# Softmax scaling moved behind the values, and heads' slots taken in twos, in an attention and expert kernel

## The chip, the cores and the metric

The kernel runs on one core of one Trainium2 chip. The metric is device time in microseconds (us). Engines in the text: PE is TensorE (PEld its weight loads), DVE is VectorE, ACT is ScalarE, POOL is GpSimd, SP is SyncE, which here only issues DMAs.

## What is computed

A block of layer norm, causal attention with 16 heads of 64 and rotary positions, and an expert layer whose output gates the attention. x is 8 x 256 x 128, all fp32.

```python
xn = layernorm(x)
q = xn @ wq.T;  lat = xn @ w_kv_down.T            # 16 heads of 64; latents of 64
k = lat @ w_k_up.T;  v = lat @ w_v_up.T
q, k = rope(q), rope(k)
probs = softmax(q @ k.T / 8 + causal)             # per head, 256 x 256
s = (probs @ v).reshape(B, S, 1024) @ wo.T
e_star = max(top2(xn @ gate_w + gate_b))          # one expert a token
g = silu(2 * (gelu(xn @ w1[e_star] + b1[e_star]) @ w2[e_star] + b2[e_star]))
out = x + s * g
```

## The kernel before, in words

The program is written engine by engine: `program` (L286) calls, on each engine, `start`, then `slot(g)` for g = 0 to 63, and between slots 39 and 40 `finish` and `experts`. The order on an engine is the order in which its functions write it; engines wait for each other by semaphores. Nothing else sets it.

A **slot** g is one pair of heads of one batch row (8 batches of 8 pairs); i in the names is the head within the pair. The 256 queries are two chunks: the first 128 (k = 0) see 128 keys, the others (k = 1) see 256. So a head's rows are 128 + 256 = 384 columns wide; the first 128 are called the corner here. In a slot:

- PE `scores(g + 2)` (L1074, L1080 for the 256 columns, L1082 for the corner) into s_bank[i]; it waits until slot g + 1's maxima are taken. The two heads lie in two halves of the rows (64*128 tiles).
- PE `project` (L1058): item m is four heads' q (m even, L1054 to L1056) or k (m odd, L1070, L1071); `items(g)` puts item g + 6 in slot g, and two of them in the slots of TWICE (36, 38).
- DVE `row_max(g + 2)` (L588, L594): mask, negated maximum and copy to `masked`, four instructions. Then `denominators(g + 1)` (L601), the reciprocal of the row sums, and `rotate` (L581, L585) of the item, which multiplies by cos and sin; POOL `rotated` (L457, L463) adds the halves into `staged`, and SP `place` (L356, L363) copies two items to `qk_sb` by four DMAs.
- ACT `exponentials(g + 1, i)` (L880, L885) with row sums, into `pexp`, double buffered.
- `scale(g + 1)` turns pexp into `probs`: four instructions, on POOL (L474), some on DVE (L612) and ACT (L898) in slots in which POOL also issues indirect DMAs.
- PE `turn(g)` (L1085, L1092): six transposes of probs into t_bank[i]; ACT `turned_probs(g)` (L901, L907) copies them to `probsT`, four slots deep.
- PE `values(g)` (L1095, L1106, L1108) multiplies by the latents into o_bank, one slot at a time up to slot 23 (`ALONE`), two slots at once after; ACT `ctx_out` (L909, L914) copies o_bank to `ctxT`; PE `output(g)` (L1111, L1120) adds the pair's share of the block's result in y_bank.
- In slots 22 to 37 POOL scatters a tile of tokens into `sorted_x` in DRAM (L482), in slots 43 to 58 it gathers the gates (L490). SP's `load` (L423, L425) brings sorted_x back into z in two pieces, 4 tiles and 18 tiles, in slot 38. DVE `finalise(b)` (L763) multiplies a batch's result by its gate and adds x, in the slots of FINALS; it reads y_keep or, from batch 5 on, y_bank.

`experts` runs 22 tiles of 128 tokens (PE L1257, L1285, L1300; ACT L1038 gelu; POOL L549 copies the expert's first weights, DVE L854 and L867). Its second tile waits for both loads of z (`t == 1`, L1295).

## Time and profile before

| | us |
|---|---|
| median of 3 runs | 309.83 (309.74 to 309.87) |
| the profiled execution | 310.5 |
| its span, first to last instruction | 308.7 |
| granted TensorE clock over the span | 0.998 |

| engine | busy us | share of the span |
|---|---|---|
| PE | 294.3 | 95% |
| PEld | 235.4 | 76% |
| ACT | 242.9 | 79% |
| DVE | 221.0 | 72% |
| POOL | 215.9 | 70% |

The chain of work that ended last is PE for 64%, POOL for 12%, DVE for 8% and ACT for 2% of the span; 11% is issue. Matmuls are pipelined: the row of one is longer than its pace, so the distance from start to start tells what it costs. A timeline row of several instructions (x4, x6) merges them. Busy time is the union of such rows.

### The profile page before, as it was taken

What the parts mean: (1) busy time and instruction counts of PE and PEld (TensorE: products, weight loads), DVE (VectorE), ACT (ScalarE), POOL (GpSimd) and SP (SyncE); (2) the same over time, 40 slices, a digit from 0 to 9 for tenths busy, and PEclk for the clock granted to TensorE, in tenths of its full rate; (3) what the DMA queues carried; (4) which work ended last, traced back from release to release, by engine and by line L of the source; (5) the groups of instructions that cost most, each with busy time, mean ns of one, the idle gap of its engine ahead of it and who ended that gap; (6) DMA issues with size and microseconds to landing.
All of it is one profiled execution on the core that took longest, in us unless ns stands there. A gap on an engine that the chain in (4) does not pass through costs nothing.

```text
span 308.7 us, 8487 instructions
## 1 busy us (share of the span) xinstructions
PE 294.3 (95%) x2362; PEld 235.4 (76%) x2362; DVE 221.0 (72%) x883; ACT 242.9 (79%) x851; POOL 215.9 (70%) x321
## 2 busy tenths in 40 slices
PE   8897999999999999999999989999989999899994
PEld 3566878888888888777777789999867777786763
DVE  3889998987787998988887523323278789898651
ACT  3387889898887889999897665555799999889982
POOL 3378878786786879999999933332138999889730
PEclk9999999999999999999999999999999999999999
DMA  6764595979333333333345470000063334344200
GB/s 204 232 140 112 107 308 124 225 168 302 74 69 71 68 71 89 92 87 87 99 104 134 129 197 0 2 2 0 3 187 71 93 102 115 103 108 133 71 19 17
DMA packets 39596, 33.35 MB, mean 108 GB/s; under 512 B 4801, under 2 KB 36674, under 8 KB 39554
## 3 DMA queue, kind: packets, MB, share of 16 engines
q1 hardware_dynamic: 38098, 30.51, 38.3%
q0 software_dynamic: 1024, 2.10, 2.5%
q8 instruction: 20, 0.33, 0.4%
q10 hardware_dynamic: 432, 0.23, 0.3%
q14 instruction: 22, 0.18, 0.2%
HBM read 11.07 MB, written 4.98 MB: 52 GB/s over the span
## 4 chain that ended last, share of the span: by engine, by line
PE 64%; POOL 12%; issue 11%; DVE 8%; ACT 2%; DMA 1%; POOLq 1%; SPq 0%; DVEq 0%; ACTq 0%
PE bank L1092 9%; PE bank L1080 8%; PE bank L1106 7%; PE bank L1120 6%; PE bank L1285 6%; PE bank L1300 6%; POOL probs L474 5%; POOL staged L463 4%; PE bank L1054 3%; DVE rot_out L585 3%; PE bank L1108 3%; PE bank L1082 3%; DVE masked L594 2%; PE bank L1188 2%; PE bank L1070 2%
## 5 line engine op out<-in xcount | busy, mean ns | idle before, releaser
L885 ACT ACTIVATE pexp<-masked,negmax 128x128 f32<-128x128 f32 (+1 forms) x256 | 114.1, 452 | 1.5 <-DVE negmax L594 1.4
L474 POOL TENSOR_SCALAR probs<-pexp,rden 128x256 f32<-128x256 f32 (+1 forms) x184 | 80.3, 451 | 26.0 <-DVE rden L601 23.3
L594 DVE CUSTOM_DVE_ANT_0 masked<-bank,mask 128x128 f32<-128x128 f32 (+1 forms) x256 | 75.9, 351 | 27.1 <-PE bank L1082 26.9
L463 POOL TENSOR_TENSOR staged<-rot_out 128x512 f32<-128x512 f32 x63 | 80.2, 1275 | 17.8 <-DVE rot_out L585 17.3
L585 DVE TENSOR_TENSOR rot_out<-bank,rot 128x1024 f32<-128x1024 f32 x64 | 77.6, 1214 | 4.0 <-PE bank L1056 2.7
L907 ACT COPY probsT<-bank 128x384 f32<-128x384 f32 x128 | 54.9, 480 | 22.9 <-PE bank L1092 21.9
L1092 PE MATMUL bank<-ident,probs 128*128 128x128 f32 x384 | 54.7, 275 | 1.8 <-ACT probsT L907 0.9
L885 ACT ACTIVATION_READ_ACCUMULATOR pexp<-masked,negmax 128x1 f32 x256 | 49.9, 195 | 0.0
L1080 PE MATMUL bank<-qk_sb 64*128 64x256 f32 x256 | 45.0, 427 | 2.9 <-DVE negmax L594 2.1
L1092 PEld LDWEIGHTS bank<-ident,probs 128*128 128x128 f32 x384 | 43.1, 140 | 5.2 <-POOL probs L474 1.9
L1120 PE MATMUL bank<-vo_sb,ctxT 128*128 128x128 f32 x256 | 39.4, 278 | 0.7 <-ACT ctxT L914 0.7
L1038 ACT ACTIVATE probsT<-bank,w_own 128x128 f32<-128x128 f32 x88 | 25.1, 367 | 18.8 <-PE bank L1285 18.8
L1106 PE MATMUL bank<-probsT,lat_all 128*64 128x256 f32 (+1 forms) x184 | 37.7, 488 | 0.3 <-ACT probsT L907 0.3
L1120 PEld LDWEIGHTS bank<-vo_sb,ctxT 128*128 128x128 f32 x256 | 33.7, 191 | 1.9 <-ACT ctxT L914 1.1
L549 POOL COPY w_own<-w_sb 128x516 f32 x22 | 13.5, 616 | 27.5 <-ACT probsT L1038 27.5
L1080 PEld LDWEIGHTS bank<-qk_sb 64*128 64x128 f32 x256 | 19.5, 184 | 16.6 <-issue 13.9
L1082 PEld LDWEIGHTS bank<-qk_sb 64*128 64x128 f32 x256 | 25.1, 187 | 2.5
L914 ACT COPY ctxT<-bank 128x256 f32<-128x256 f32 (+1 forms) x46 | 20.8, 451 | 6.9 <-PE bank L1108 5.6
L1300 PE MATMUL bank<-w_sb,probsT 128*128 x176 | 24.4, 282 | 0.8 <-issue 0.5
L1082 PE MATMUL bank<-qk_sb 64*128 64x128 f32 x256 | 25.0, 271 | 0.0
L1108 PEld LDWEIGHTS bank<-probsT,lat_all 128*64 128x64 f32 x184 | 13.3, 137 | 14.3 <-issue 10.3
L1285 PE MATMUL bank<-probsT,w_own 128*128 128x128 f32 x176 | 23.4, 276 | 0.7 <-DVE probsT L854 0.4
(113 smaller groups left out, 458.1 us busy)
## 6 DMA issues: line engine op xcount, KB each, us to landing
qk_sb<-staged SPq DMA_DIRECT2D x128, 128.0 KB, 2.5
w_sb<-in_w SPq DMA_DIRECT2D x2, 1024.0 KB, 5.6
w_sb<-in_w SPq DMA_DIRECT2D x4, 512.0 KB, 4.9
sorted_x<-z SPq DMA_DIRECT2D x1, 1408.0 KB, 7.9
sorted_g<-z SPq DMA_DIRECT2D x1, 1152.0 KB, 5.5
out<-res SPq DMA_DIRECT2D x8, 128.0 KB, 1.8
x_sb<-in_x SPq DMA_DIRECT2D x3, 256.0 KB, 3.8
rot<-in_c_rot SPq DMA_DIRECT2D x1, 512.0 KB, 5.0
```

Source lines behind the costliest of these rows:

```text
L463: pool.tensor_tensor(staged[:, n % 2, :, m % 2, :], rot_out[:, m % 2, :, 0:S], rot_out[:, m % 2, :, S:2 * S], op=ALU.add).then_inc(staged_ ...
L474: pool.tensor_scalar(probs[:, g % 2, i, c], pexp[:, g % 2, i, c], rden[:, g % 2, i, k:k + 1], 1.0, ALU.mult, ALU.mult).then_inc(probs_read ...
L585: dve.tensor_tensor(rot_out[:, m % 2], bank_of(m)[:].unsqueeze(1).broadcast_to([P, 2, 2 * S]), rot[:], op=ALU.mult).then_inc(rope_done, 1)
L594: t = dve.tensor_tensor_reduce(masked[:, g % 2, i, c], s_bank[i][:, c], mask[:, c], -1.0, -NEG * 1e8, ALU.add, ALU.min, negmax[:, g % 2, i ...
L885: e = act.activation(pexp[:, g % 2, i, c], masked[:, g % 2, i, c], ACT.Exp, bias=negmax[:, g % 2, i, k:k + 1], scale=-1.0, accum_out=rowsu ...
L907: act.copy(probsT[:, g % 4, i, :], t_bank[i][:, 0:SW]).then_inc(probsT_ready, 1)
L1080: pe.matmul(s_bank[i][:, P:SW], qk_sb[r, 0, p, P:S], qk_sb[r, 1, p, :], start=True, stop=True)
L1082: m = pe.matmul(s_bank[i][:, 0:P], qk_sb[r, 0, p, 0:P], qk_sb[r, 1, p, 0:P], start=True, stop=True)
L1092: t = pe.transpose(t_bank[i][:, k * P:(k + 1) * P], probs[:, g % 2, i, k * P:(k + 1) * P], ident[:])
L1106: pe.matmul(o[r, :, :], lat_all[:, 2 * b, :], probsT[:, pairs, i, 0:S], start=True, stop=False)
L1120: m = pe.matmul(y_bank[:, i * C:(i + 1) * C], ctxT[:, p, i * P:(i + 1) * P], vo_sb[:, p, :], start=(p == 0 and i == 0), stop=(p == NP - 1) ...
L1300: m = pe.matmul(bank[6 + i][:, 0:C], hidT[:, i, k, :], w2_sb[:, k, :, :].rearrange("p e c -> p (e c)")[:, bass.ds(e * C, C)], start=(k == ...
```

## The change

From slot 24 on, slots are taken in **couples** (24 and 25, 26 and 27, ...). Each engine has a `couple(g)` for even g that stands in place of slot(g) and slot(g + 1).

- PE writes the scores of two slots at once: the 256-column parts side by side in s_bank, the corners in t_bank, the bank of the transposes. So a transpose waits until DVE has read both corners (`corner_read`), and the corners wait until ACT has copied the last transposes.
- DVE takes the corners' maxima (`corner_max`) and the rest (`rest_max`) apart.
- `pexp` is transposed unscaled (but for slots 38, 39, 62 and 63, which DVE and POOL scale in place). The reciprocals of a couple, 8 columns, are transposed by PE within turn(g), copied to SBUF by ACT, written by SP to DRAM (`rows_out`) and read back as rows spread over 64 partitions for either head (`rows_back`), into the space of probs. DVE's new `ctx_out` multiplies them into o_bank's 512 columns; ACT's copy is gone from slot 24 on.
- `values` of slots 38, 39, 62 and 63 go in twos as well; values(38) uses s_bank[1].
- TWICE is (23, 25). The second load of z is issued after the placing in couple 38, and has its own semaphore `xs_rest`.

```diff
-TWICE = (36, 38)
+TWICE = (23, 25)
...
             def slot(g):
-                if g == G_LEAD - 2:
-                    sp.wait_ge(scattered, 16 * NT)
-                    load(0, 4)
-                    sp.wait_ge(xs_in, 16)
-                    load(4, NR)
...
@@ SP @@
+            def couple(g):
+                if g == G_LEAD - 2:
+                    sp.wait_ge(scattered, 16 * NT)
+                    load(0, 4, xs_in)
+                if not scaled(g):
+                    rows_out(g // 2)
+                    rows_back(g // 2)
+                for m in (*items(g), *items(g + 1)):
+                    if m % 2:
+                        place(m // 2)
+                if g == G_LEAD - 2:
+                    load(4, NR, xs_rest)
...
@@ POOL @@
+            def couple(g):
+                if scaled(g + 1):
+                    scale(g + 1)
+                for n in range(g, g + 2):
+                    for m in items(n):
+                        rotated(m)
+                    if SCATTER_SLOT <= n < SCATTER_SLOT + NT:
+                        scatter(n - SCATTER_SLOT)
...
+                if g < LAST and scaled(g + 2):
+                    scale(g + 2)
...
+            def corner_max(g):
+
+                dve.wait_ge(scores_done, g + 1)
+                dve.wait_ge(exp_done, 2 * g - 6)
+                for i in range(2):
+                    t = dve.tensor_tensor_reduce(corner(g, i), t_bank[i][:, g % 2 * P:(g % 2 + 1) * P], mask[:, 0:P],
+                                                 -1.0, -NEG * 1e8, ALU.add, ALU.min, negmax[:, g % 4, i, 0:1])
+                t.then_inc(corner_read, 1)
...
@@ DVE @@
+            def ctx_out(g):
+
+                u = g // 2
+                dve.wait_ge(pv_done, values_through(g))
+                dve.wait_ge(y_step, g + 2 - NP)
+                o, heads = v_bank(g)[:, 0:2 * S], ctxT[:, g % NP:g % NP + 2, :].rearrange("p n s -> p (n s)")
+                if scaled(g):
+                    dve.tensor_copy(heads, o).then_inc(ctx_ready, 1)
+                else:
+                    dve.wait_ge(row_in[u % 2], 32 * sum(n % 2 == u % 2 for n in units(u)))
+                    dve.tensor_tensor(heads, o, shares[:, u % 2].rearrange("p n s -> p (n s)"),
+                                      op=ALU.mult).then_inc(ctx_ready, 1)
+
@@ DVE @@
+            def couple(g):
+                if g - 4 >= FIRST_DOUBLE and g not in (G_LEAD, G_LEAD + 2):
+                    ctx_out(g - 4)
+                if g < LAST:
+                    corner_max(g + 2)
+                    corner_max(g + 3)
+                denominators(g + 1)
+                if scaled(g + 1):
+                    scale(g + 1)
+                if g < LAST:
+                    rest_max(g + 2)
+                for m in items(g):
+                    rotate(m)
...
+                if FINALS.get(g + 1, -1) >= LEAD:
+                    finalise(FINALS[g + 1])
+                if g < LAST:
+                    rest_max(g + 3)
+                    denominators(g + 2)
+                if g < LAST and scaled(g + 2):
+                    scale(g + 2)
+                for n in range(g, g + 2):
+                    if FINALS.get(n, LEAD) < LEAD:
+                        finalise(FINALS[n])
+                if g in (G_LEAD - 2, LAST):
+                    ctx_out(g - 2)
+                for m in items(g + 1):
+                    rotate(m)
...
@@ ACT @@
+            def couple(g):
...
+                turned_probs(g)
+                if g < LAST:
+                    exponentials(g + 2, 0)
+                    if g != G_LEAD - 2:
+                        exponentials(g + 2, 1)
+                turned_probs(g + 1)
+                if g == G_LEAD - 2:
+                    exponentials(g + 2, 1)
+                if g < LAST:
+                    for i in range(2):
+                        exponentials(g + 3, i)
...
             def turn(g):
 
+                wait(pe, corner_read, corners_through(g + 3 - g % 2))
                 for i in range(2):
                     wait(pe, probsT_ready, 2 * g + i - 1)
+                    if not scaled(g):
+                        pe.wait_ge(exp_done, 2 * g + i + 1)
+                    if i and g % 2 == 0 and not scaled(g):
+                        pe.wait_ge(rden_ready, g + 2)
+                        pe.transpose(t_bank[1][0:8, SW:SW + P], rden[:, g // 2 % 2].rearrange("p n i k -> p (n i k)"), ident[:])
...
@@ PE @@
+            def couple(g):
+                ahead = (*items(g), *items(g + 1))
+                if g < LAST:
+                    scores_of_two(g + 2)
+                for m in ahead[:2]:
+                    project(m)
+                if ahead:
+                    turn(g)
...
+                elif g not in (G_LEAD, G_LEAD + 2):
+                    output(g - 4)
+                    output(g - 3)
+                if not ahead:
+                    turn(g)
+                if g == LAST:
+                    values(g - 2)
+                turn(g + 1)
...
+                elif g not in (G_LEAD, LAST):
+                    values(g - 2)
+                if g == G_LEAD - 2:
+                    values(g)
...
-                            pe.wait_ge(xs_in, 32)
+                            pe.wait_ge(xs_rest, 16)
```

PE in two slots of the middle. Before, from one values to the next outputs (L1080 and L1082 are scores, L1070 to L1071 and L1054 to L1056 projections, L1092 transposes, L1120 outputs):

```order
L1108 MATMUL bank<-probsT,lat_all 64x2x128 x2
L1080 MATMUL bank<-qk_sb 128x256 x2
L1082 MATMUL bank<-qk_sb 128x128 x2
L1070 MATMUL bank<-latT,wk_h 128x256
L1071 MATMUL bank<-latT,wk_l 128x256
...
L1092 MATMUL bank<-ident,probs 128x128 x6
L1120 MATMUL bank<-vo_sb,ctxT 128x128 x2
L1080 MATMUL bank<-qk_sb 128x256 x2
L1082 MATMUL bank<-qk_sb 128x128 x2
L1054 MATMUL bank<-xnT_h,wq_h 128x256
```

Now (L1231 and L1236 are the scores, L1253 the transposes, L1249 that of the reciprocals, L1285 outputs, L1271 values):

```order
L1231 MATMUL bank<-qk_sb 128x256 [waits qk_in0,masked_ready]
...
L1236 MATMUL bank<-qk_sb 128x128 [waits probsT_ready]
...
L1209 MATMUL bank<-latT,wk_h 128x256 [waits rope_done]
...
L1253 MATMUL bank<-ident,pexp 128x128 [waits exp_done,probsT_ready,corner_read]
L1253 MATMUL bank<-ident,pexp 128x128 x2
L1249 MATMUL bank<-ident,rden 8x128 [waits rden_ready,exp_done,probsT_ready]
L1253 MATMUL bank<-ident,pexp 128x128 x3
L1285 MATMUL bank<-vo_sb,ctxT 128x128 [waits ctx_ready,y_read]
```

Two rounds of scores, projection and transposes, each with its own output, became one round of both slots' scores and both projections, one transpose, both outputs and the other transpose.

SP ahead of the experts, before:

```order
L363 DMA qk_sb<-staged 64x2x256 x3
L425 DMA z<-sorted_x 128x4x128 [waits scattered]
L425 DMA z<-sorted_x 128x18x128 [waits xs_in]
L363 DMA qk_sb<-staged 64x2x256 [waits scores_done,staged_ready]
L363 DMA qk_sb<-staged 64x2x256 x3
```

and now (L414 is place, L476 load, L526 the gates' way out):

```order
L414 DMA qk_sb<-staged 64x2x256 x3
L476 DMA z<-sorted_x 128x4x128 [waits scattered]
L414 DMA qk_sb<-staged 64x2x256 [waits scores_done,staged_ready]
L414 DMA qk_sb<-staged 64x2x256 x3
L476 DMA z<-sorted_x 128x18x128
L526 DMA sorted_g<-z 128x18x128 [waits g_ready]
```

The second load moved behind the placing of items 46 and 47.

DVE in couple 38, from the rest of slot 41's maxima to the experts (L711 reciprocal, L958 multiplication, L675 rotation, L955 copy of slots 38 and 39, L1003 the experts' first copy):

```order
L701 ISA masked,negmax<-bank,mask 128x256
L701 ISA negmax 128x1
L711 RECIPROCAL rden<-rowsum 128x4 [waits probsT_done,exp_done]
L958 TENSOR_TENSOR ctxT<-bank,probs 128x512 [waits row_in0,y_step,pv_done]
L675 TENSOR_TENSOR rot_out<-bank,rot 128x1024 [waits staged_ready,proj_done]
L955 COPY ctxT<-bank 128x512 [waits y_step,pv_done]
L1003 COPY probsT<-bank 128x128 [waits fb_in,xsT_done,tile_ready]
```

The same place before (L601 reciprocal, L585 rotation, L761 the block's result to y_keep):

```order
L594 ISA masked,negmax<-bank,mask 128x256
L594 ISA negmax 128x1
L601 RECIPROCAL rden<-rowsum 128x4 [waits exp_done]
L585 TENSOR_TENSOR rot_out<-bank,rot 128x1024 [waits staged_ready,proj_done]
L854 COPY probsT<-bank 128x128 [waits fb_in,xsT_done,tile_ready]
L601 RECIPROCAL rden<-rowsum 128x4 [waits exp_done]
L761 COPY y_keep<-bank 128x256 [waits y_step]
```

The last rotation ahead of the experts stood behind slot 39's reciprocal alone; now it stands behind that of slot 40 and the multiplication of slots 36 and 37.

## Rows read from the trace of the kernel before

**Rows 1.** Windows by stretch: busy us of PE, PEld, DVE, ACT, POOL; clock, DMA.

```profile
115.51:176.65 61.14, 60.36 (x470) 46.69 (x468) 49.66 (x182) 52.63 (x194) 57.95 (x75) 1.00 0.39 99
...
222.93:236.01 13.08, 11.97 (x90) 8.97 (x89) 9.10 (x41) 12.71 (x37) 7.28 (x12) 1.00 0.52 140
236.01:278.43 42.42, 41.63 (x325) 32.48 (x324) 37.32 (x141) 38.35 (x139) 38.17 (x47) 1.00 0.39 103
278.43:308.75 30.32, 25.30 (x189) 17.79 (x188) 15.90 (x74) 23.04 (x83) 15.37 (x25) 0.98 0.21 56
144.30:151.23 6.93, 6.93 (x57) 5.40 (x56) 5.81 (x23) 6.36 (x25) 6.51 (x9) 1.00 0.36 97
```

**Rows 2.** Timeline of PE in two slots: start us, us, engine, line, operation, tiles.

```profile
146.94 0.70 PE L1080 MATMUL bank<-qk_sb 64*128 64x256 f32 x4
147.47 0.39 PE L1082 MATMUL bank<-qk_sb 64*128 64x128 f32 x4
147.79 0.39 PE L1070 MATMUL bank<-latT,wk_h 128*128 128x256 f32 x1
...
148.37 0.82 PE L1092 MATMUL bank<-ident,probs 128*128 128x128 f32 x6
149.02 0.61 PE L1120 MATMUL bank<-vo_sb,ctxT 128*128 128x128 f32 x4
149.56 0.70 PE L1080 MATMUL bank<-qk_sb 64*128 64x256 f32 x4
...
150.41 0.38 PE L1054 MATMUL bank<-xnT_h,wq_h 128*128 128x256 f32 x1
...
151.23 0.82 PE L1092 MATMUL bank<-ident,probs 128*128 128x128 f32 x6
```

**Rows 3.** Timeline of ACT in the same slots.

```profile
150.00 0.40 ACT L885 ACTIVATE pexp<-masked,negmax 128x128 f32<-128x128 f32 x1
...
150.87 0.39 ACT L885 ACTIVATE pexp<-masked,negmax 128x128 f32<-128x128 f32 x1
...
152.09 0.86 ACT L907 COPY probsT<-bank 128x384 f32<-128x384 f32 x2 [0.23 <-PE bank L1092]
```

**Rows 4.** Timeline of DVE in the same slots.

```profile
147.91 0.29 DVE L594 CUSTOM_DVE_ANT_0 masked<-bank,mask 128x128 f32<-128x128 f32 x1 [0.91 <-PE bank L1082]
...
149.03 0.17 DVE L601 RECIPROCAL rden<-rowsum 128x4 f32<-128x4 f32 x1
...
149.44 1.22 DVE L585 TENSOR_TENSOR rot_out<-bank,rot 128x1024 f32<-128x1024 f32 x1
150.57 0.28 DVE L594 CUSTOM_DVE_ANT_0 masked<-bank,mask 128x128 f32<-128x128 f32 x1
```

**Rows 5.** Groups by line and form: count, busy us, mean ns, idle before.

```profile
L463 POOL TENSOR_TENSOR staged<-rot_out 128x512 f32<-128x512 f32 x63 | 80.2, 1275 | 17.8 <-DVE rot_out L585 17.3 <-PE bank L1092 0.2
...
L474 POOL TENSOR_SCALAR probs<-pexp,rden 128x256 f32<-128x256 f32 x124 | 59.7, 486 | 1.9 <-DVE rden L601 0.4
...
L482 POOL DMA_INDIRECT sorted_x<-xn,pos x16 | 17.2, 1077 | 2.7 <-issue 2.3 <-PE bank L1092 0.3
...
L644 DVE TENSOR_TENSOR xnT_l<-bank,xnT_h 128x512 fp32r<-128x512 f32 x3 | 2.0, 682 | 0.0
```

**Rows 6.** Timeline of DVE at the end of the span, last finalisation.

```profile
305.60 0.42 DVE L769 TENSOR_TENSOR gated<-bank,xn 128x256 f32<-128x256 f32 x1 [5.42 <-PE bank L1120]
```

**Rows 7.** Lines L363 and L425, SP's issues (ns), and L425's times to landing.

```profile
L363 SPq DMA_DIRECT2D qk_sb<-staged x128: 590/608/2276, 12.8 to 283.8; - x128
...
DMA to landing us min/median/max: 2.8/4.9/7.0
```

**Rows 8.** Timeline of PE: the experts' first group, and tile 1's second.

```profile
176.65 1.13 PE L1285 MATMUL bank<-probsT,w_own 128*128 128x128 f32 x8 [0.29 <-POOL w_own L549]
...
182.04 1.06 PE L1300 MATMUL bank<-w_sb,probsT 128*128 x8
```

**Rows 9.** Timeline of ACT at slot 40, behind the experts.

```profile
226.43 1.28 ACT L885 ACT_TABLE_LOAD   x1
```

245 lines of the change are left out of this document (147 added, 98 removed).

## The prediction

> **What bounds the kernel now.** After the page's busy shares, in the table above, which say PE, I read the busy time by stretch, for slots 24 to 39, the experts' restart, the slots with projections after it, and the tail [rows 1]. In two slots of the middle (144.30 to 151.23, all that two slots take) PE has 6.93 busy us in 6.93, POOL 6.51, ACT 6.36, DVE 5.81: PE sets the pace and three engines run just under it. Only the tail has much idle PE time: 25.30 busy in 30.32. Then the order of time of PE, to see what a slot is made of [rows 2], and of ACT and DVE [rows 3, 4].
>
> PE, start to start [rows 2]: scores 0.85 (146.94 to 147.79), k projection 0.58, transposes 0.65, output 0.54, q projection 0.82. One pass over 256 columns of scores costs 0.21, over 128 columns 0.11; the rest of the 0.85 is some 0.11 when the tile shape goes to 64*128 and as much when it goes back. A projection that follows another would lose its own first 0.11 too.
> By the Trainium skill (TensorEngine Tiling (Array Packing), Key Properties) changing the tiling mode drains TensorE; the trace agrees.
>
> **The change part by part.**
> 1. *Scores in twos.* A couple has one change to 64*128 and back in place of two: 1.50 for four heads against 2 x 0.85, so -0.20. q and k in a row: -0.11. Both outputs between transposes: -0.09, since one change from output to scores goes. Added: a transpose of the reciprocals, 0.11 (a sixth of the 0.65). Sum: 6.93 - 0.40 + 0.11 = 6.64 a couple, -0.29. The new transpose is 8 columns wide; were it another tile shape it would cost up to 0.11 more on each side, 0.32. I take 0.11, the nearest row, and keep the other end for a rival.
> 2. *POOL* loses the scaling, in all of these stretches. Being under PE, that alone buys nothing but room: two rotations of 1.28 and two indirect DMAs of about 1.1 in 6.64.
> 3. *ACT* loses its output copies and scaling, gains a copy of 8x128 a couple. The nearest row has 0.86 for two copies of 384 columns [rows 3], 0.37 start to start; 128 columns take no more than that and no less than 0.1, I take 0.2. ACT's couple: four heads at 0.87 (150.00 to 150.87) [rows 3] = 3.5, four copies at 0.37 = 1.5, 0.2: 5.2. Not the bound.
> 4. *DVE* loses its scaling (0.2 a slot) and gains the multiplication from PSUM, 128x512: the nearest row is 0.68 [rows 5], 0.60 start to start; not under 0.5, not over 0.7. Couple: maxima 2 x 1.12, two rotations of 1.13 [rows 4], 0.6, 0.2 = 5.3. Under 6.64, but now it is a chain. From the start of transpose g: the transposes 0.76, their read-out by ACT until the second copy is issued 0.8, the two heads of g+2 1.85 with the last accumulator read, reciprocal 0.1 to the next start, rotation 1.13 (149.44 to 150.57), multiplication 0.6, four corner maxima of 128x128 at 0.21 with the last read 0.9 (a slot's four maxima of both widths take 1.12, 147.91 to 149.03 [rows 4]), and only then may transpose g+2 overwrite the corners, which stand in its bank: 6.2, with the hand-overs between engines of 0.05 each 6.4. It fits with 0.25 to spare. A third rotation in a couple (couple 24, where projections are moved to) doesn't fit: 1.0 wait in couple 26. A finalisation placed after the reciprocal doesn't either: 0.42 for its first half [rows 6] and no less for the second, 0.85 together, so 0.6 of wait in each couple with one.
> 5. *The round trip of the reciprocals.* Three issues on SP a couple, 0.6 each at most, and two landings, one after the other, of 4 KB and 2 x 128 KB, at 2.8 or less, what the first load of z, 256 KB, takes [rows 7]; the multiplication is two couples (13 us) after the transpose. Hidden. SP's queue: 1.8 + 4 x 0.61 [rows 7] of 6.64.
>
> **Sum by stretch**, against the profiled span.
> *Slots 23 to 39.* The q projection moved to slot 23 costs 0.90 there. Then couples 24 and 26: 5.9 and 7.2 (1.0 of it the wait above); four at 6.7; couple 36 to its transpose 3.0. PE begins slot 24 at 115.51, the edge of the first window [rows 1], so transpose 36 stands at 115.5 + 0.9 + 42.8 = 159.2. I count from there. The exponentials of 38 end at 3.5; DVE's reciprocal and its scaling of one head of 38 end at 4.3, its rotation of item 45 at 5.5. POOL then rotates 45 (1.28 [rows 5], to 6.8), issues the scatter of tile 15 (1.08 [rows 5] and a gap, to 8.0) and only then scales the other head of 38 (two instructions, the wider 0.49 [rows 5], 0.85 together, to 8.9): transpose 38 ends at 9.2, where PE alone would be at 7.3, a wait of 1.9. ACT: copies of 38 to 9.8, the first head of 40 to 10.7, copies of 39 (transposed at 10.7, since two outputs stand between) to 11.4, the second head of 40 to 12.4. DVE, in its own order: reciprocal 40, multiplication 36 (to 13.2), rotation 47 (to 14.4). POOL rotates 47: X = 15.7. Its first copy of expert weights, for which PE waits today too [rows 8], lets the experts start at X + 0.7 = 16.4, so at 175.6, 1.0 before the 176.65 of today.
> *The load.* On SP the load of sorted rows 4 to 21 now stands behind the placing of items 46 and 47, which waits for that last rotation, and costs four issues of 0.61. It goes out at X + 2.6 and lands 7.0 later [rows 7]: X + 9.6. The second matmul group of the experts (tile 1) waits for it, today 5.4 after the first [rows 8]; it would be ready at X + 6.1. Wait 3.5. In absolute time tile 1 goes on at 159.2 + 25.3 = 184.5 in place of 182.04: **+2.4**. The rest of the experts is PE's own pace and gives nothing back.
> By the Trainium skill (DMA: Bandwidth & Descriptors, Anatomy of one DMA), whose fit of a fixed 2.0 us and the bytes over 436 GB/s is for POOL's path, 1.18 MB would take an estimated 4.7 us and the wait would be 1.2; the row says 7.0.
> *Restart.* Counted from PE's start of slot 40, 222.93: scores and projections end at 2.8, the transpose of 40 at 3.6. ACT, done with its silu by then, copies 40 to 4.4, loads the exponential table, 1.28 [rows 9], does both heads of 42 to 7.5 and only then the copies of 41, to 8.3. The corners of couple 42 go into that bank, so they wait until 8.35; today slot 44's scores have a bank of their own. Projections then end at 10.2, transpose 42 at 11.0, transpose 43, behind the copies of 42, at 12.3, values 40 at 13.8. Today slot 44 begins at 13.08, the length of that window [rows 1]: **+0.7**.
> *Slots 44 to 55.* Six couples at 6.64 to 6.75 and three waits of 0.6 for late finalisations, 42.3 against 42.42: **-0.1**.
> *Tail.* Without projections nothing covers ACT and DVE. A couple is ACT's loop: copies 0.9, exponentials 1.8, copies 0.75, exponentials 1.8, reciprocal 0.1, the half transpose and its read-out 0.8: 6.15. Couples 56, 58, 60: 6.9, 6.2, 6.2. The first is 6.9 because couple 54 leaves DVE late, by finalisation and rotation. Couple 62 starts on PE at 19.3. On DVE the exponentials of 62 end at 19.1, then reciprocal, scaling of 62 (0.6) and finalisation 4 (0.85) stand before multiplication 58, which is ready only at 21.4: PE has nothing else and waits 2.1. Two outputs 0.9, transpose 62 0.65, values 60 with its change of shape 1.5, transpose 63 0.65: 25.2. Multiplication 60 is ready by then; two outputs to 26.2, values 62 (both slots at once, 1.5) to 27.7, DVE's copy of 512 columns to 28.5, two outputs to 29.6. Then 3.1 as today, from the last finalisation at 305.60 to the end at 308.7 [rows 6]. 32.7 against 30.32: **+2.4**.
> Together +5.4, less 0.2 for work that PE finds in its waits: span 308.7 + 5.2. The profiled execution took 310.5, the median of the timed runs is 309.83; so 309.8 + 5.2 = **315.0**.
>
> **Rivals.**
> *PE alone decides* (0.18). The chains fit and the load is not waited for: twelve couples at -0.29 is -3.5, a little more where PE idles today: 306, range 305 to 308.5. For it: PE is at 100% of the middle stretch and every other engine loses work. Against: the load's place in SP's queue and the late scaling on POOL can be read off the order; it decides only if the load lands 3.5 sooner.
> *Half of it* (0.12). The load is waited for, but the tail holds today's time: 309 to 312.
> *The other way out* (0.20). The narrow transpose changes the tile shape, 0.2 more a couple, and that lengthens ACT's and DVE's chain too: 11 x 0.2 = 2.3 on top, 317.5.
> *The stated saving isn't on the path* (within my forecast). POOL's scaling goes, but POOL is not what PE waits for in [rows 1]; so the change can do all it says and be slower.
> My forecast has 0.50: 312 to 317.
>
> **How the numbers follow.** A measurement of this kernel tells about 0.2% from no change, 0.6 us. Faster: the first rival and a trace of the second, 0.19. Within: 0.06 from the second. Slower: 0.75. The range 308.5 to 319 leaves out most of the first rival (0.17) and a few per cent above.
>
> **What would show it.** Right: a couple of 6.6 to 6.8 in slots 28 to 36; an idle PE of 2 to 4 us before the second group of W2 matmuls of tile 1; a PE wait for POOL's pexp in slot 38; PE idle of 1 or more before the outputs of couple 62. Wrong: the z load landed before tile 1; couples over 6.9 (then the narrow transpose or the chain, to be told by whether PE idles); a tail under 31.

## The result, and the profile after

| | before | after |
|---|---|---|
| median of 4 runs, us | 309.85 (309.74 to 310.61) | 318.94 (317.08 to 320.54) |
| span of the profiled execution | 308.7 | 316.7 |
| granted TensorE clock over the span | 0.998 | 0.986 |
| busy share of PE, ACT, DVE, POOL | 95, 79, 72, 70% | 92, 71, 69, 56% |

The ratio is 1.0286, 95% interval 1.0228 to 1.0344: slower, by 9.1 us. POOL lost 40 us of work, ACT 19, and none of it shows in the time.

Windows of the changed kernel, columns as in [rows 1], in the order of time: start of the experts to tile 1's second group, from there to slot 40, restart, slots 44 to 55, tail, one couple of the middle, and two stretches that are new.

```profile
175.29:184.44 9.15, 4.66 (x35) 3.96 (x36) 1.18 (x5) 3.43 (x12) 2.27 (x4) 1.00 0.78 186
184.44:226.89 42.45, 42.12 (x338) 39.76 (x338) 11.10 (x38) 22.92 (x77) 10.49 (x17) 0.96 0.01 2
184.74:188.15 3.41, 3.41 (x18) 3.41 (x17) 0.29 (x1) 0.14 (x1) 0.00 (x0) 0.50 0.02 5
226.89:242.32 15.43, 12.77 (x88) 9.67 (x87) 8.88 (x41) 12.46 (x37) 3.82 (x3) 0.89 0.54 147
235.94:239.35 3.41, 3.41 (x18) 3.33 (x17) 3.29 (x17) 1.26 (x7) 1.51 (x2) 0.50 0.40 126
242.32:283.25 40.93, 40.39 (x332) 31.79 (x330) 35.20 (x134) 31.89 (x128) 26.73 (x24) 1.00 0.52 140
283.25:316.70 33.45, 25.78 (x189) 17.39 (x187) 17.73 (x76) 19.52 (x76) 7.76 (x10) 0.97 0.30 84
142.59:149.24 6.65, 6.65 (x57) 5.29 (x55) 5.41 (x22) 5.26 (x22) 4.51 (x5) 1.00 0.50 141
```

The last row is what the change was to bring: 6.65 where [rows 1] has 6.93 for two slots, and POOL down from 6.51 to 4.51. The first row is what it cost: 9.15 with 4.66 of PE work, where the kernel before needs 5.39 (176.65 to 182.04, [rows 8]). The third and fifth rows were in nobody's sum: for 3.41 us each the granted clock is 0.50, that is 1.2 GHz in place of 2.4, once 0.3 behind the start of tile 1's group, which ends the wait there, and once 0.7 behind the end of a wait of 2.0 at the restart. The kernel before has a low clock only in its last 1.4 us, behind PE's last work, and the changed kernel has that one too.

The order of time of PE in one couple, around the new transpose, and at tile 1, where the last column shows the wait:

```profile
142.59 1.14 PE L1231 MATMUL bank<-qk_sb 64*128 64x256 f32 x8
...
145.40 0.49 PE L1253 MATMUL bank<-ident,pexp 128*128 128x128 f32 x3
145.72 0.27 PE L1249 MATMUL bank<-ident,rden 128*8 128x128 f32 x1
145.83 0.49 PE L1253 MATMUL bank<-ident,pexp 128*128 128x128 f32 x3
```

```profile
178.51 1.15 PE L1484 MATMUL bank<-w_sb,probsT 128*128 x8 [0.33 <-issue]
179.50 1.06 PE L1469 MATMUL bank<-probsT,w_own 128*128 128x128 f32 x8
180.39 0.27 PE L1441 MATMUL bank<-ident,z 128*128 128x128 f32 x1
184.44 1.82 PE L1484 MATMUL bank<-w_sb,probsT 128*128 x8 [3.78 <-issue]
186.05 1.92 PE L1469 MATMUL bank<-probsT,w_own 128*128 128x128 f32 x8
```

The transpose of the reciprocals (L1249, 128*8) costs 0.11 from start to start and nothing at its sides. At tile 1 the same group takes 1.15 before the wait and 1.82 behind it.

SP's issues in the same stretch, placing and load (start, duration, line):

```profile
174.41 2.55 SPq L414 DMA_DIRECT2D qk_sb<-staged  x4
177.41 0.75 SPq L476 DMA_DIRECT2D z<-sorted_x  x1
```

The load goes out behind the four placings and lands 6.8 later.

### The profile page after: what moved, and what is told of

It reads as the page before. It is cut to its first block, busy times and chain, and to the rows that moved or that the text cites. A ratio compares the mean times of both kernels' runs of the same rounds, so it can differ in the third digit from the quotient of the medians.

```text
span 316.7 us, 8321 instructions
## 1 busy us (share of the span) xinstructions
PE 292.5 (92%) x2364; PEld 234.7 (74%) x2364; DVE 218.5 (69%) x873; ACT 223.8 (71%) x815; POOL 176.0 (56%) x239
## 4 chain that ended last, share of the span: by engine, by line
PE 70%; DVE 11%; issue 8%; ACT 5%; DMA 2%; SPq 2%; POOL 1%; DVEq 0%; POOLq 0%; ACTq 0%
PE bank L1253 11%; PE bank L1484 7%; PE bank L1271 7%; PE bank L1285 7%; PE bank L1469 7%; PE bank L1231 4%; PE bank L1219 4%; PE bank L1193 4%; DVE rot_out L675 4%; ACT pexp L1036 3%; PE bank L1273 3%; DMA z<-in_woT 2%; PE bank L1195 2%; PE bank L1194 2%; DVE masked L684 2%
## 5 line engine op out<-in xcount | busy, mean ns | idle before, releaser
L1036 ACT ACTIVATE pexp<-masked,negmax 128x128 f32<-128x128 f32 (+1 forms) x216 | 98.2, 458 | 1.5 <-DVE negmax L684 1.4
L675 DVE TENSOR_TENSOR rot_out<-bank,rot 128x1024 f32<-128x1024 f32 x64 | 77.6, 1215 | 2.3 <-PE bank L1195 1.9
L551 POOL TENSOR_SCALAR probs<-pexp,rden 128x128 f32<-128x128 f32 x94 | 38.5, 428 | 16.3 <-DVE rden L711 16.0
L1036 ACT ACTIVATION_READ_ACCUMULATOR pexp<-masked,negmax 128x1 f32 x216 | 41.3, 191 | 0.0
L1285 PE MATMUL bank<-vo_sb,ctxT 128*128 128x128 f32 x256 | 37.0, 280 | 3.8 <-DVE ctxT L958 2.9
L1253 PE MATMUL bank<-ident,pexp 128*128 128x128 f32 x240 | 37.5, 279 | 2.8 <-POOL pexp L551 1.1
L684 DVE CUSTOM_DVE_ANT_0 masked<-bank,mask 128x128 f32<-128x128 f32 x104 | 30.9, 353 | 11.1 <-PE bank L1221 11.0
L1271 PE MATMUL bank<-probsT,lat_all 128*64 128x256 f32 (+1 forms) x176 | 37.2, 501 | 0.0
L1285 PEld LDWEIGHTS bank<-vo_sb,ctxT 128*128 128x128 f32 x256 | 32.2, 191 | 6.5 <-DVE ctxT L958 4.1
L1253 PEld LDWEIGHTS bank<-ident,pexp 128*128 128x128 f32 x240 | 27.8, 143 | 7.5 <-ACT probsT L1051 2.8
L701 DVE CUSTOM_DVE_ANT_0 masked<-bank,mask 128x256 f32<-128x256 f32 x76 | 28.4, 413 | 0.0
L711 DVE RECIPROCAL rden<-rowsum 128x4 f32<-128x4 f32 x64 | 11.2, 175 | 24.8 <-ACT pexp L1036 24.6
L1484 PEld LDWEIGHTS bank<-w_sb,probsT 128*128 128x128 f32 x176 | 22.1, 197 | 7.1 <-issue 7.1
L1193 PE MATMUL bank<-xnT_h,wq_h 128*128 128x256 f32 x64 | 21.4, 335 | 2.0 <-DVE rot_out L675 1.7
```

The lines of the kernel that those rows point to most:

```text
L551: pool.tensor_scalar(scaled_to(g)[:, i, c], pexp[:, g % 2, i, c], rden[:, g // 2 % 2, g % 2, i, k:k + 1], 1.0, ALU.mult, ALU.mult).then_in ...
L675: dve.tensor_tensor(rot_out[:, m % 2], bank_of(m)[:].unsqueeze(1).broadcast_to([P, 2, 2 * S]), rot[:], op=ALU.mult).then_inc(rope_done, 1)
L684: t = dve.tensor_tensor_reduce(masked[:, g % 2, i, c], s_bank[i][:, c], mask[:, c], -1.0, -NEG * 1e8, ALU.add, ALU.min, negmax[:, g % 4, i ...
L1036: e = act.activation(pexp[:, g % 2, i, c], masked[:, g % 2, i, c] if k else corner(g, i), ACT.Exp, bias=negmax[:, g % 4, i, k:k + 1], scal ...
L1193: pe.matmul(o, lh, rh, start=start, stop=False)
L1253: t = pe.transpose(t_bank[i][:, k * P:(k + 1) * P], (probs if g < FIRST_DOUBLE else pexp)[:, g % 2, i, k * P:(k + 1) * P], ident[:])
```

## The experiments

Each edit is to the changed kernel unless said otherwise, and each kernel does all the work of the reference. They ran in four groups, each on one chip beside the kernel before, whose median was 310.4 to 310.7 in all of them. The changed kernel was timed again in the second of them (experiments 6, 7 and 8); what is said against it of experiments 1 to 5, 9, 10 and 11 is a difference across chips. For the changed kernel, timed again:

> The changed kernel as it is, once more, beside the edits of this call, since its times spread over 317.1 to 320.5. My theory: two things differ from run to run, how much PE work falls into the 3.4 us of low clock behind each wait, and whether the multiplication of heads 54 waits for its reciprocals (1.4 to 1.6 in three of the edited kernels, not in the one profile of the changed kernel). Median 318.9 (318 to 320), both to be seen in the profile or not. Rival: the spread has another source, and the profile shows the same waits with other lengths.

319.30 (318.38 to 321.55), ratio 1.0291 (1.0250 to 1.0331). Its profile repeats the first within 0.3 in each stretch: the wait at tile 1 is 3.74, the low clock lasts 3.41 twice, and heads 54 did not wait. What its times spread by is taken up under the third and the sixth experiment.

**1. The second load back in its place.**

```diff
                 if g == G_LEAD - 2:
                     sp.wait_ge(scattered, 16 * NT)
                     load(0, 4, xs_in)
+                    sp.wait_ge(xs_in, 16)
+                    load(4, NR, xs_rest)
...
                         place(m // 2)
-                if g == G_LEAD - 2:
-                    load(4, NR, xs_rest)
```

> The changed kernel, with the load of sorted rows 4 to 21 put back where the kernel before has it on SP's queue: directly behind the landing of the first load, ahead of the placing of the last keys and queries. My theory: in the changed kernel this load goes out at 177.4 and lands 6.8 later, PE stands 3.8 us before the second group of tile 1 (184.44), and right behind that wait the granted clock is 0.5 for 3.4 us (184.7 to 188.2), which costs 1.6 more up to slot 40. With the load out at about 172 it lands before 179.5: the wait is under 0.3, tile 1's group starts at 180.7, the clock stays at 1.0 there. 318.9 - 3.8 - 1.6 = 313.5 (312.5 to 314.5). Rival 1, the low clock comes from denser work on PE in slots 24 to 39 and not from the wait: only the wait goes, the clock still falls near 185, 315.2. Rival 2, the load is held up by the exchange of reciprocals and the indirect transfers, and lands late wherever it is issued: over 317.

315.82 (314.88 to 316.70), 3.5 under the changed kernel's 319.30 and over the expected 314.5. Windows of this kernel, of the same work as the first two rows above:

```profile
175.86:181.09 5.23, 4.49 (x35) 4.02 (x36) 0.88 (x4) 2.29 (x8) 1.65 (x3) 1.00 0.88 249
181.09:222.12 41.03, 40.64 (x341) 38.07 (x339) 11.39 (x39) 24.07 (x81) 11.11 (x18) 1.00 0.01 2
```

9.15 became 5.23 and 42.45 became 41.03, with the clock at 1.00: -3.9 for the wait and -1.4 for the clock, as expected, and against both rivals. The time came down less than these 5.3, since this profile lies 0.6 behind that of the changed kernel already at PE's first scores (17.53 against 16.96), long before the edit acts, and couple 58 takes 1.3 more, on which more below.

**2. The same fault in the kernel before.**

```diff
                     sp.wait_ge(xs_in, 16)
-                    load(4, NR)
                 for m in items(g):
                     if m % 2:
                         place(m // 2)
+                if g == G_LEAD - 1:
+                    load(4, NR)
```

> The kernel before, with one edit: its second load of sorted rows is issued behind the placing of the last keys and queries instead of ahead of it. My theory: the loss at tile 1 hangs on this place alone, and not on slots in twos or unscaled transposes. The last rotation ends at 175.9, four issues take 2.5, so the load goes out at 178.5 and lands 7.0 later, 185.5, where tile 1's group stands at 182.04: a wait of 3.5. The low clock follows the wait as in the changed kernel: 1.6 more. 309.8 + 3.5 + 1.6 = 314.9 (313.8 to 315.6). Rival 1, a low clock belongs to the changed kernel's denser work: 313.3. Rival 2, the load is not what tile 1 waits for: 309.8.

317.07 (316.34 to 317.61), 6.5 over the kernel before. The place of one DMA issue, with nothing else changed, costs seven tenths of what the whole change costs. Windows of it:

```profile
176.10:185.67 9.57, 4.66 (x35) 3.96 (x36) 1.53 (x6) 4.57 (x13) 3.87 (x8) 0.95 0.79 195
184.75:191.58 6.83, 5.91 (x27) 5.91 (x28) 0.58 (x2) 1.14 (x4) 0.62 (x1) 0.50 0.01 3
185.67:229.27 43.60, 43.35 (x340) 41.02 (x340) 11.09 (x38) 22.94 (x77) 10.49 (x17) 0.93 0.01 2
```

The wait is 4.2 more than before (9.57 against 5.39), and the low clock begins inside it and lasts 6.83, so it costs 2.7 (43.60 against 40.89). Expected were 3.5 and 1.6, and a time of 315.6 at most. The low clock is no matter of the changed kernel's denser work.

**3. The gap filled with work.** 16 multiplications whose results nobody reads stand on PE ahead of the wait.

```diff
                         if t == 1:
-                            pe.wait_ge(xs_rest, 16)
                             pe.wait_ge(y_read, LEAD)
+                            keep_warm(16, bank[6 + i])
+                            pe.wait_ge(xs_rest, 16)
```

> The changed kernel, with 16 multiplications of 512 columns, whose results nobody reads, put on PE just ahead of its wait for the second load (about 0.21 us each at the full clock, 3.4 us, from 180.7 to 184.1). The load comes no sooner. My theory: the clock falls at 184.7 because PE stood idle before. With the gap filled it stays at 1.0 through the experts: tile 1's group starts at 184.4 as before, and slot 40 begins 1.6 sooner, span 316.7 - 1.6 = 315.1, time 317.3 (317.0 to 317.8). Rival 1, the clock falls for the density of the work before it: it falls at the same place or sooner, time 318.9 or more. Rival 2: the filling itself takes longer than the gap, over 319.

PE at tile 1 in this kernel, and two windows, one of them where the changed kernel has its low clock:

```profile
180.07 3.62 PE L1353 MATMUL bank<-ones 128*128 128x512 bf16 x16
183.88 1.15 PE L1485 MATMUL bank<-w_sb,probsT 128*128 x8 [0.20 <-DMA z<-sorted_x]
```

```profile
183.88:224.74 40.86, 40.56 (x338) 38.16 (x338) 11.10 (x38) 22.93 (x77) 10.49 (x17) 1.00 0.01 1
184.70:188.20 3.50, 3.50 (x33) 3.45 (x33) 0.94 (x4) 1.33 (x5) 0.62 (x1) 1.00 0.00 0
```

The load is still late, and goes out 0.44 sooner than in the changed kernel only because this whole profile lies that much ahead; so the group starts at 183.88 in place of 184.44. But its row is 1.15 again and the experts take 40.86 in place of 42.45: the clock alone is worth 1.6, and what brings it down is that PE stood idle. The filling took 3.62 and fitted into the gap. The releaser of the wait is now named too, the DMA of z. The time was 319.42 (318.48 to 320.27) all the same, not 317.3: it lies where both rivals had it, though neither of their reasons is in the rows. The profile has two losses further on that the changed kernel's has not: 1.4 in couple 58, and a low clock of 3.41 in the tail:

```profile
304.92:308.33 3.41, 3.41 (x14) 1.85 (x15) 0.02 (x1) 0.96 (x2) 0.36 (x1) 0.50 0.05 13
```

This is the likeliest source of the spread, and was not tested by itself. The waits recur to 0.1 from kernel to kernel, but how long the clock stays low behind them does not, and of the changed kernel's runs the one of 320.54 had a mean granted clock of 0.984, those of 318.94 had 0.986 and 0.989, and the one of 317.08 had 0.995. It isn't the only source: of experiment 1's runs the one of 314.88 had 0.991 and the one of 315.32 had 0.995.

By the Trainium skill (TensorE: Matmul & The Clock Gate, HAM oscillation) a wait for a DMA between groups of multiplications lets the clock fall, so that the next group starts at the low one. The trace agrees, here with fp32 groups and a wait of 3.2 to 4.2, but for the moment: the clock fell from 1.6 before the end of the wait to 1.0 behind it.

**4. ACT's copies first, at the restart.**

```diff
                 turned_probs(g)
+                if g == G_LEAD:
+                    turned_probs(g + 1)
                 if g < LAST:
                     exponentials(g + 2, 0)
...
-                turned_probs(g + 1)
+                if g != G_LEAD:
+                    turned_probs(g + 1)
```

> The changed kernel, with one change of ACT's order at the restart behind the experts: the copies of transpose 41 ahead of the exponentials of 42. My theory: the corner scores of slots 44 and 45 wait 2.0 (to 235.25, 8.4 behind the start of slot 40) for these copies. They would then be done at about 5.8, the exponentials of 42 at 8.9 behind a table load of 1.28, those of 43 at 10.7, the copies of 42 at 11.5, transpose 43 at 12.1 in place of 14.1: 1.5 to 2.0 faster, and the fall of the clock at 235.94 gone, which is worth 0 to 0.3 here, since ACT sets the end. 318.9 - 1.8 = 317.1 (316.6 to 317.6). Rival: the exponentials of 42 are what the rest hangs on, so what the corners gain, transpose 42 loses: within 0.4 of 318.9.

321.10 (320.45 to 321.75), over the expected 317.6 and over the changed kernel; couple 44 begins 15.43 after slot 40, to the hundredth what it was. The profile's span is 1.5 longer, all of it in couple 58, which takes 7.72 in place of 6.23 (see experiment 6). PE's order of time in couple 42, first of the changed kernel, then of this one:

```profile
232.08 1.13 PE L1231 MATMUL bank<-qk_sb 64*128 64x256 f32 x8 [0.19 <-DVE negmax L701]
235.25 0.71 PE L1236 MATMUL bank<-qk_sb 64*128 64x128 f32 x8 [2.04 <-ACT probsT L1051]
```

```profile
233.24 0.39 PE L1239 MATMUL bank<-qk_sb 64*128 64x128 f32 x4
...
236.93 0.58 PE L1212 MATMUL bank<-latT,wk_h 128*128 128x256 f32 x1 [2.40 <-DVE rot_out L675]
```

The wait for ACT is gone, and one for DVE took its place: the k projection may only run when the rotation of the item before is done, and that stands on DVE behind the reciprocal of 42, which needs the exponentials that now come later. The theory named one of two queues. The clock fell here too, at 236.53, inside the new wait.

**5. Both queues.** On top of 4, DVE's second rotation of couple 40 goes ahead of the reciprocal of 42.

```diff
                     rest_max(g + 3)
+                if g == G_LEAD:
+                    for m in items(g + 1):
+                        rotate(m)
+                if g < LAST:
                     denominators(g + 2)
...
-                for m in items(g + 1):
+                for m in items(g + 1) if g != G_LEAD else ():
                     rotate(m)
```

> The changed kernel, with two moves at the restart behind the experts: on ACT the copies of transpose 41 ahead of the exponentials of 42 (that alone took the corners' wait of 2.0 away and put one of 2.4 on DVE's rotation in its place, at the projections of couple 42), and on DVE the second rotation of couple 40 ahead of the reciprocal of 42, which waits for the exponentials. My theory: that rotation stood behind the reciprocal 42, and so behind the exponentials 42. With both moved the scores and projections of couple 42 run through, transpose 43 stands at 12.1 to 12.8 from the start of slot 40 in place of 14.1, couple 44 begins 13.5 to 14.3 from it in place of 15.4: 1.1 to 1.9 faster, and no low clock at 235: 318.9 - 1.5 = 317.4 (316.9 to 318.0). Rival: ACT's own chain (table load, four heads, four copies) is as long in any order: couple 44 begins 15.0 or later, 318.5 or more.

321.57 (320.60 to 324.09), with couple 44 16.1 after slot 40: the expectation fell, and so would the theory, were it not for the clock. The profile is of the slowest of the four runs; the fastest lies over the changed kernel too. The same two moves are in the kernel of experiment 9, where couple 44 begins 14.0 after slot 40, as was expected. Their couple 42, first here, then there:

```profile
233.42:244.34 10.92, 8.91 (x48) 5.42 (x48) 6.10 (x22) 9.97 (x37) 3.64 (x4) 0.72 0.57 155
```

```profile
227.65:236.50 8.85, 6.36 (x48) 4.38 (x48) 4.97 (x22) 8.31 (x30) 3.18 (x3) 1.00 0.71 189
```

In both PE waits 1.68 ahead of transpose 42; here the clock falls behind it for 6.83 and the couple takes 10.92, there it stays at 1.00 and the couple takes 8.85, against 10.24 in the changed kernel, with its low clock of 3.41. So the moves, in the one profile in which the clock held, are worth 1.4 together with the clock, and in the other a low clock took more than that back. Both profiles are of one run each.

**6. Stores in SP's wait.**

```diff
                     rows_out(g // 2)
+                for n in (g - 2, g - 1):
+                    if n in FINALS:
+                        store(FINAL_ORDER.index(FINALS[n]))
+                if not scaled(g):
                     rows_back(g // 2)
...
-                for n in (g, g + 1):
-                    if n in FINALS:
-                        store(FINAL_ORDER.index(FINALS[n]))
```

> The changed kernel, with each store of a finished batch moved on SP's queue from behind the placing into the couple after it, between the reciprocals' way out and their way back, where SP stands 2.1 to 2.5 us for the landing anyway. My theory: with a store, SP's couple is 7.0 us (reciprocals out 0.4, wait for their landing 2.2, back 1.25, placing 2.6, store 0.6) against 6.64 on PE; SP falls behind from couple 50 on, and in some runs the multiplication of heads 54 waits for that, 1.4. With the store inside the wait SP's couple is 6.5: no such wait. 318.9 - 0.7 = 318.2 (317.2 to 318.8), less spread. Rival: the 1.4 comes from slow landings of the reciprocals (five indirect gathers run at the same time), not from SP's queue: nothing changes.

319.53 (317.37 to 321.03), the same as the changed kernel's 319.30. SP did get faster: the reciprocals went out every 6.9 to 7.1 in place of 7.2 to 7.8. It bought nothing, as the rival had it. The wait of couple 58 was there in every kernel with this chain in the first and third group (experiments 1, 3, 4, 5, 9) and in none of the second and fourth, with and without the edit, so this pair can't show it. What speaks for the landing: in experiment 1 the reciprocals of 54 left SP 6.8 before couple 58 began, and DVE waited for them,

```profile
287.42 0.69 DVE L958 TENSOR_TENSOR ctxT<-bank,probs 128x512 f32<-128x512 f32 x1 [1.42 <-remote]
```

while in the second profile of the changed kernel they left 6.1 before it, later, and no one waited.

**7. Heads 58 first, in the tail.**

```diff
-                if g - 4 >= FIRST_DOUBLE and g not in (G_LEAD, G_LEAD + 2):
+                if g - 4 >= FIRST_DOUBLE and g not in (G_LEAD, G_LEAD + 2, LAST):
                     ctx_out(g - 4)
...
                     rest_max(g + 3)
+                    if g == LAST - 2:
+                        ctx_out(g - 2)
                     denominators(g + 2)
```

> The changed kernel, with the multiplication of heads 58 moved on DVE from behind finalisation 4 to ahead of reciprocal and scaling of 62. My theory: PE stands 2.16 before the outputs of couple 62 (304.78), since the multiplication starts at 304.05 and could start when values 58 are done, 302.6, plus a hand-over. It now starts there: the wait falls to 0.8, transposes 62 find their scaling done behind two outputs of 1.16: 1.3 faster. 318.9 - 1.3 = 317.6 (317.2 to 318.2). Rival: the path through reciprocal, scaling on POOL and transpose 62 is as long, since these now wait for the multiplication: within 0.4 of 318.9.

317.30 (317.05 to 318.00), 2.0 under the changed kernel beside it. PE before the outputs of couple 62, in the changed kernel and here:

```profile
304.78 1.16 PE L1285 MATMUL bank<-vo_sb,ctxT 128*128 128x128 f32 x8 [2.16 <-DVE ctxT L958]
```

```profile
303.28 1.16 PE L1287 MATMUL bank<-vo_sb,ctxT 128*128 128x128 f32 x8 [0.79 <-DVE ctxT L958]
```

2.16 to 0.79, and the stretch from couple 60's start to the end came down from 20.4 to 19.0: -1.4 as expected, no part of it taken back by transpose 62. The other 0.6 of the medians no row shows.

**8. Finalisations ahead of the reciprocal.**

```diff
                     rest_max(g + 3)
+                    for n in range(g, g + 2):
+                        if FINALS.get(n, LEAD) < LEAD:
+                            finalise(FINALS[n])
                     denominators(g + 2)
                 if g < LAST and scaled(g + 2):
                     scale(g + 2)
-                for n in range(g, g + 2):
-                    if FINALS.get(n, LEAD) < LEAD:
-                        finalise(FINALS[n])
```

> The changed kernel, with the finalisations of batches 1 to 4 moved on DVE from behind the reciprocal of g+2 to ahead of it, where DVE idles 0.9 to 2.1 us for ACT's exponentials. My theory: a finalisation (0.8) behind the reciprocal lengthens the chain of DVE and ACT from 6.4 to 7.2, and PE waits for it: couples 50 and 54 take 7.33 and 7.02 against 6.64, couple 56 6.84 against 6.2 and couple 62 waits for finalisation 4 too (0.85 of its 2.16). 54 and 56 come down by 0.4 and 0.6, couple 62 by 0.8; 50, of which a half is the finalisation of batch 5 that stays, by 0 to 0.3: 318.9 - 1.9 = 317.0 (316.2 to 317.8). Rival: DVE has no idle time there, what is moved delays the reciprocal by as much: within 0.4 of 318.9.

316.36 (314.68 to 316.63), 2.9 under the changed kernel. Couples 50, 54 and 56 take 6.83, 6.65 and 6.30 where they took 7.33, 7.02 and 6.84, together -1.4, and couple 62 waits 1.29 in place of 2.16. Another 0.4 is in couple 42 (9.84), which the edit does not touch: the clock falls 0.7 later in it. The edit holds one more line, by which a finalisation waits for the one before it. The chain of DVE and ACT is what the small waits came from, and what stands behind the reciprocal is in it while what stands ahead of it is not.

**9. All of them.** Experiments 1, 5, 6, 7 and 8 together, and on POOL the scaling of 38 ahead of rotation 45 and scatter 15.

> The changed kernel with all the moves that worked, and three smaller ones: second load ahead of the placing (-5.3), multiplication 58 and the finalisations ahead of the reciprocals (together -3.2), copies and rotation at the restart (-1.5), stores in SP's wait (0), and on POOL the scaling of 38 ahead of rotation 45 and the scatter (-0.5; PE waits 1.05 there, of which the late rotation takes back a part). Every piece of work is still done, only its place in the queues differs. My theory: the losses are at separate places and add up: 318.9 - 10.5 = 308.4 (307.2 to 309.8), 0.5% under the kernel before, which is the -0.29 a couple that PE's count gives, less slot 23 and the tail. Rival: they overlap, or the moved work delays what stood there: 310.5 to 313, slower than before still.

311.74 (310.88 to 314.14), ratio to the kernel before 1.0054 (1.0027 to 1.0081). That is over the expected 309.8 and in the range of the rival. Of the 10.5 it gains 7.6, against 319.30. Of the 2.9 that are missing, couple 58 takes 1.4 more than in the changed kernel (7.61 against 6.23, with a wait of 1.0), and POOL's scaling gave none of its 0.5: moved, it let transpose 38 go at once, and transpose 39 waited 0.93 in its place, behind the same rotation and scatter, as the rival says of moved work. The remaining 1.0 is in small pieces, 0.5 of it ahead of PE's first scores.

**10. All of them, the last gathers later.** As 9, without POOL's move; the gathers of tiles 14 and 15 wait for transposes 58 and 59 (shown here), and the corners of 44 and 45 are read ahead of the reciprocal of 42.

```diff
                 pool.wait_ge(g_out, 32)
+                if n in GATHER_ORDER[-2:]:
+                    pool.wait_ge(probsT_done, 2 * (G_LEAD + 19 + n % 2))
```

> All moves together again, with three differences. First, POOL issues the last two gathers, of tiles 14 and 15, whose rows only the last finalisation reads, behind transposes 58 and 59 and no longer one after the other at the end of the rotations. My theory: the wait of 1.0 to 1.4 before the outputs of couple 58 (heads 54 wait for their reciprocals, issued 6 us before) comes from the DMA engines: with all moves together they are at 0.86 to 0.95 from 280 to 283, when four gathers, four placings, a store and the reciprocals meet, and SP's order did not help. With two gathers fewer there, the share falls and the wait is gone: couple 58 takes 6.2 to 6.4 in place of 7.6. Second, the scaling of 38 stands where the changed kernel has it, since its move only carried the wait from one slot to the next. Third, at the restart the corners of 44 and 45 are read ahead of the reciprocal of 42: 0.3 to 0.8 off couple 42's 8.84. Sum: 311.7 - 1.2 - 0.5 = 310.0 (309.2 to 311.0), about the time of the kernel before. Rival: the wait at couple 58 is the two landings one after the other and stays, 311.2 or more.

310.39 (308.78 to 311.92), ratio 0.9990 (0.9966 to 1.0014): the same as the kernel before. Three of its twelve runs, of 308.78, 308.97 and 309.11, had a mean granted clock of 0.999 and lie under all seventeen of the kernel before, of which the lowest took 309.73; the nine others had 0.989 to 0.994 and took 310.21 to 311.92. The DMA share of the 3 us in which the reciprocals of 54 are under way, first in 9, then here:

```profile
280.00:283.00 3.00, 2.77 (x19) 1.23 (x19) 1.52 (x7) 3.00 (x12) 2.09 (x4) 1.00 0.89 239
```

```profile
280.00:283.00 3.00, 2.77 (x18) 1.26 (x16) 1.63 (x9) 2.96 (x12) 1.24 (x2) 1.00 0.73 198
```

The share fell and couple 58 took 6.23 with no wait. That this is the cause stays open: the changed kernel had 0.84 at the same distance into couple 56 (286.65 to 289.65) and did not wait, experiment 1 had 0.42 (281.81 to 284.81) and did, and this kernel ran in a group of its own. Its low clock came back at the restart, behind a wait of 2.32, and couple 42 took 10.20 again: 1.4 that 9 did not lose. Behind that fall it can't be told whether the third move gave its 0.3 to 0.8.

**11. Slots in twos with scaled exponentials.** What do the unscaled transposes do for the couples?

```diff
 def scaled(g):
 
-    return g < FIRST_DOUBLE or g in (G_LEAD - 2, G_LEAD - 1, LAST, LAST + 1)
+    return True
```

DVE scales the first head of 24 too, and the turn from POOL to both engines stands at 24 in place of 38.

> The changed kernel, with slots in twos but every exponential scaled in place by DVE and POOL before its transpose (as the changed kernel does for slots 38, 39, 62, 63), so no reciprocals are transposed, sent round or multiplied in; DVE copies the heads. It tells what the unscaled transposes are worth to slots in twos. My theory: scaling puts DVE's 0.6 for one head and POOL's 0.85 for the other, behind its rotations of 1.28, into the chain between exponentials and transpose: of 6.64 a couple in slots 28 to 36 not much is left, 7.4 to 8.5, since POOL scales the first slot of the next couple behind two rotations. 12 couples at +1.3: 318.9 + 15 = 334 (326 to 342). Rival: there is room enough in the chain, a couple stays under 6.9 and loses 0.11 by the missing transpose: 318.

340.33 (339.66 to 344.49). One couple of the middle, and in it the wait of PE and what POOL did:

```profile
148.15:156.22 8.07, 6.97 (x56) 5.23 (x54) 6.43 (x26) 5.20 (x22) 6.19 (x8) 1.00 0.32 83
```

```profile
152.51 0.79 PE L1255 MATMUL bank<-ident,pexp 128*128 128x128 f32 x3 [1.04 <-ACT probsT L1053]
```

```profile
150.96 0.98 POOL L560 DMA_INDIRECT sorted_x<-xn,pos  x1 [0.16 <-issue]
151.99 1.62 POOL L551 TENSOR_SCALAR pexp<-pexp,rden 128x128 f32<-128x128 f32 x4
```

The row puts the wait down to ACT; but the second head's transposes also wait for POOL's scaling, behind a rotation and a scatter. Its corner is done at 152.36 and PE starts at 152.51; its 256 columns are done at 152.81 and PE goes on at 152.87. 8.07 against 6.65: without the unscaled transposes slots in twos lose 1.1 to two slots of the kernel before. The half of the change that looked like a cost, 0.11 and a round trip through DRAM, is what makes the other half possible, at least with this order on POOL; scaling ahead of rotation and scatter in every couple was not tried.

## Why the prediction was right, and by how much it missed

315.0 was predicted, 318.94 measured, slower as forecast and by the mechanisms named: all four signs under "Right" are in the rows. The number was inside the range of 308.5 to 319 by 0.06, and that is luck: the same kernel timed again took 319.30, the loss was 9.1 where 5.2 was forecast, and 318.94 lies over the 312 to 317 that the forecast gave itself and over the sum of every rival. The steps against the first profile:

| step | predicted | measured |
|---|---|---|
| a couple in slots 28 to 36 | 6.64 | 6.65 |
| couples 24 and 26 together | 13.1 | 13.1 |
| wait for POOL's scaling of 38 | 1.9 | 1.05 |
| the experts start | 175.6 | 175.29 |
| wait at tile 1 | 3.5 | 3.78 |
| tile 1 goes on | 184.5 | 184.44 |
| from there to slot 40, against 40.89 of before | 0 | +1.56 |
| restart, from slot 40 to couple 44 | 13.8 | 15.43 |
| slots 44 to 55 | 42.3 | 40.93 |
| tail: couples 56, 58, 60 | 6.9, 6.2, 6.2 | 6.84, 6.23, 6.3 |
| tail: wait for multiplication 58 | 2.1 | 2.16 |
| tail in all, 283.25 to the end | 32.7 | 33.45 |
| span | +5.2 | +8.0 |

(The sum's 13.8 is the end of values 40, where couple 44 starts: transpose 43 ends at 12.3 in it, and values take 1.5.)

*Scores in twos.* Right to 0.01, with all its parts: one change of tile shape fewer, q and k in a row, and 0.11 for the narrow transpose. The rival of another tile shape falls with the rows at 145.72 and 145.83, though its 317.5 was the number nearest to the result.

*The step that was wrong* is "The rest of the experts is PE's own pace and gives nothing back". It takes more: PE's pace behind a wait of 3.8 is not its pace before it. 1.56 of the 2.8 that the span missed are there, and experiments 1 and 3 show the cause from two sides, by taking the wait away and by filling it.

*The restart* was missed by as much, 1.6. The corners of couple 42 start at 8.36, where the sum had 8.35. Then PE's work falls into the low clock of 235.94 to 239.35: the projections end at 11.3, not 10.2, and transpose 43 at 14.0, not 12.3. It is PE that sets the pace there, and ACT waits for it:

```profile
239.11 0.48 ACT L1051 COPY probsT<-bank 128x384 f32<-128x384 f32 x1 [2.15 <-PE bank L1253]
```

So a fall of the clock was missing from the sum twice. No run has this order of work at the restart without it, so its share of the 1.6 is read from the rows and not shown by an experiment.

*Slots 44 to 55* hid this in the total, by luck. The sum took couples of up to 6.75 and three waits of 0.6; in the rows four couples take 6.64 or 6.65, and couples 50 and 54 take 0.7 and 0.4 more: 1.4 less than was summed.

*The tail* is 0.75 longer than the sum. In couple 62 two outputs behind the wait cost 1.0 to 1.2, not 0.9, which makes 0.5 up to the last outputs; the other 0.2 lie behind them, in a stretch that was taken over from [rows 6]. The 0.2 that PE was to find in its waits it did not find. 1.56, 1.6, -1.4, 0.75 and 0.2 make 2.7 of the 2.8.

*From span to time.* The sum was added to the median 309.8, which lies 1.1 over the span of before; the changed kernel's median lies 2.2 over its span. That is the other 1.1 of the 3.9 between 315.0 and 318.94. The profiled execution of before, at 310.5, already stood 0.7 over the median, and was the better base.

*SP's queue* was put at 4.2 of 6.64. The wait for the first landing, 2.1 from the issue at 160.75 to the next at 162.85, blocks the queue too, and with a store SP's couple is 7.0. It did no harm that a run shows, but "hidden" was worked out without it; the chain over the landings did cost 1.0 to 1.6 in five kernels.

*POOL's scaling of 38* made PE wait half as long as in the sum. The start of the experts hangs on it as the sum says, through ACT's copies and exponentials, the reciprocal of 40 at 171.10 and the last rotation, and came 0.3 sooner than predicted.

*The rivals.* That PE alone decides would have needed a load that lands 3.5 sooner. That the tail holds its time is refuted by its 33.45; the sum without the tail's +2.4 gives 312.6, over the 309 to 312 that this rival was given. Experiment 10 comes nearest to the first of them, with the load not waited for and the other waits shortened, and took 310.4 where that rival has 306. The couples' gain is there, 59.6 from 115.51 to the start of the experts against 61.1, and 40.1 in slots 44 to 55 against 42.4. Slots in twos lose it at the restart, 15.4 against 13.1, and in the tail, 31.6 against 30.3 of [rows 1], even without any of the misplaced work. So the best form of the change that was found equals the kernel before in the median, and is 0.6 or more under every run of it only in the three of twelve in which the clock hardly fell.

*Small slips of the sums.* 5.9, 7.2, four times 6.7 and 3.0 make 42.9, not 42.8, and 315.0 and 2.3 make 317.3, not 317.5. Neither moves the forecast.
